# One edge-message kernel on Trainium2: the segment sums are issued ahead of the edge products on TensorE, and one wait goes

## The reference

```
h   = max(layernorm(x), 0)                        # 12500 x 48
tmp = concat([h[dst], h[src], edge_attr], 1)      # 400000 x (48 + 48 + 32)
msg = relu(tmp @ W1 + b1) @ W2 + b2               # hidden width 128
x  += segment_sum(msg, dst, num_segments=12500)
```

## Time and profile before

| | |
|---|---|
| median of three runs | 4776.21 us (4758.83 to 4780.47) |
| the profiled execution's own time | 4776.21 us |
| its span | 4774.3 us |
| TensorE busy, share of the span | 82% |
| GpSimd busy, share of the span | 55% |
| VectorE, ScalarE busy | 54%, 43% |
| mean granted TensorE clock, share of full | 0.85 |

### The profile page before, as it was taken

One profiled execution on the slowest core, in us unless ns is written; L12 is line 12 of the kernel. 1 busy time (PEld: TensorE's weight loads), 2 busy tenths in 40 slices (PEclk: granted clock), 3 DMA queues, 4 the chain that ended last, 5 costly groups with the idle time before them and its releaser, 6 DMA issues.

```text
span 4774.3 us, 95161 instructions
## 1 busy us (share of the span) xinstructions
PE 3927.4 (82%) x21992; PEld 3397.9 (71%) x21992; DVE 2554.6 (54%) x5906; ACT 2043.4 (43%) x7414; POOL 2613.2 (55%) x2766
## 2 busy tenths in 40 slices
PE   3788888888888888888888888888888888888887
PEld 3677777777777777777777777777777777777776
DVE  3655555565555555555555555555555555555553
ACT  2444444444444444444444444444444444444443
POOL 5455555555555555555555555555555555555555
PEclk9988888888888888888888888888888888888886
DMA  4522222222222222222222222222222222222223
GB/s 146 142 80 72 75 78 79 78 78 75 76 77 76 78 74 75 76 78 76 76 75 74 77 77 77 76 76 73 77 74 77 75 77 73 78 75 79 74 79 81
DMA packets 286658, 380.47 MB, mean 80 GB/s; under 512 B 90916, under 2 KB 190549, under 8 KB 285542
## 3 DMA queue, kind: packets, MB, share of 16 engines
q0 software_dynamic: 88064, 177.91, 14.7%
q1 hardware_dynamic: 198342, 201.58, 14.6%
q10 hardware_dynamic: 208, 0.49, 0.1%
HBM read 362.58 MB, written 17.04 MB: 80 GB/s over the span
## 4 chain that ended last, share of the span: by engine, by line
another core or an unknown queue 30%; issue 19%; DVE 18%; PE 14%; DVEq 11%; SPq 4%; ACT 4%; DMA 1%; ACTq 0%
PE ps L1310 6%; DVEq L1004 5%; DVE lhs L992 5%; PE ps L1286 3%; PE ps L1294 3%; DVE gath L1001 2%; DVE work L1047 2%; DVE onehot L979 2%; DVE p_hot L1025 2%; ACT work L674 2%; DVE nodes L1014 2%; SPq L411 1%; SPq L412 1%; DVEq L1093 1%
## 5 line engine op out<-in xcount | busy, mean ns | idle before, releaser
L535 POOL DMA_INDIRECT gath<-b_table,idx x2688 | 2549.3, 948 | 2127.3 <-ACT idx L639 1294.6
L1310 PE MATMUL ps<-h_tab,p_hot 128*128 128x480 f32 (+1 forms) x6768 | 1944.0, 431 | 259.5 <-issue 255.7
L1310 PEld LDWEIGHTS ps<-h_tab,p_hot 128*128 128x128 f32 x6768 | 1449.9, 226 | 467.6 <-issue 344.3
L674 ACT ACTIVATE work<-ps,work 128x80 f32<-128x80 f32 x4136 | 1039.1, 408 | 1675.3 <-remote 1458.2
L1286 PE MATMUL ps<-rhs,lhs 96*128 96x128 f32 x5376 | 906.6, 316 | 270.1 <-DVE gath L1001 124.3
L1286 PEld LDWEIGHTS ps<-rhs,lhs 96*128 96x128 f32 x5376 | 785.3, 219 | 403.1 <-issue 331.8
L1014 DVE TENSOR_TENSOR nodes<-ps,nodes 48x48 f32 x768 | 153.7, 200 | 1611.5 <-remote 1490.1
L1294 PE MATMUL ps<-onehot,gath 128*128 128x48 f32 x5376 | 799.6, 295 | 88.4 <-ACT gath L655 75.0
L1294 PEld LDWEIGHTS ps<-onehot,gath 128*128 128x128 f32 x5376 | 783.1, 221 | 109.1 <-ACT gath L655 95.0
L1025 DVE TENSOR_TENSOR p_hot<-work,ps 128x1152 fp32r<-128x1152 f32 x376 | 506.6, 1347 | 57.7 <-PE ps L1310 34.0
L992 DVE TENSOR_SCALAR_CACHE_REDUCE lhs<-nodes 48x512 f32<-48x512 f32 (+1 forms) x768 | 520.0, 677 | 32.0 <-issue 5.7
(11 more groups left out here) (128 smaller groups left out, 1640.8 us busy)
## 6 DMA issues: line engine op xcount, KB each, us to landing
nodes<-dst_row SPq DMA_DIRECT2D x494, 96.0 KB
gath<-b_table,idx POOLq DMA_INDIRECT x2688
nodes<-dst_row SPq DMA_DIRECT2D x384, 72.0 KB
lhs<-in_edge_t SPq DMA_DIRECT2D x384, 64.0 KB
work<-key_row SPq DMA_DIRECT2D x94, 256.0 KB
lhs<-in_edge_t SPq DMA_DIRECT2D x384, 48.0 KB
rhs<-a_table SPq DMA_DIRECT2D x768, 24.0 KB
work<-in_edge_t SPq DMA_DIRECT2D x220, 32.0 KB
```

The lines of the kernel that those rows point to most:

```text
L535: pool.indirect_dma_start(gath[:, u, t, :], None, b_table, bass.IndirectOffsetOnAxis(ap=idx[:, u, t:t + 1], axis=0)).then_inc(gathered[u], 16)
L674: m = nc.scalar.activation(p_sel[:, t % 2, :, at_j], ps_run[:, q, j * words:(j + 1) * words], ACT.Copy, scale=p_mask[:, at_j, t:t + 1])
L1310: mm = nc.tensor.matmul(ps_run[:, q, 0:m * words].rearrange("p (j w) -> p j w", j=m), p_hot[:, t % 2, i, :], h_tab[:, first:first + BLOCKS ...
```

## The change

On TensorE alone: in every step `make_sums` is issued ahead of `make_z` instead of behind it, and so are `make_sums_tail` of the early tiles and `turn_p` where j is 3. `make_z` no longer waits for `z_added`: `make_sums` of the same step, now ahead of it, waits for `r_ready` of the same step two before, which ScalarE signals after it has waited for that `z_added`.

```
@@ make_z
                 pe.wait_ge(hott_ready, s + 1)
-                if k >= 2:
-                    pe.wait_ge(z_added, s - 1)
                 for t in range(step_tiles(k)):
@@ cycle
                     k = LEAD + c * PERIOD + j
-                    make_z(k - 1, it)
                     make_sums(k - 3, it)
                     if j == 3 and ends_e:
                         make_sums_tail(place_e(c - 1, it))
                     if j == 3 and not first:
                         turn_p(c - 1, it)
+                    make_z(k - 1, it)
                     if j == 1 and ends_e:
                         make_z_tail(place_e(c - 1, it))
@@ after the last cycle
             for k in range(fetched, fetched + 3):
+                make_sums(k - 3, 0)
                 if k == fetched:
                     make_z(k - 1, 0)
-                make_sums(k - 3, 0)
                 if k % 2 == 0:
                     fold(k - 3, 0)
```

## The result

The changed kernel takes 4955.5 us (median of four runs, 4940.9 to 4962.33), the kernel before 4778.34 us beside it (4758.83 to 4783.35): 1.0394 of before, 95% interval 1.0348 to 1.0442, so 3.9% slower. The forecast was 4910 us with a range of 4765 to 5000. The profiled execution of after is on the long side: 4993.92 us with a span of 4992.1, where the thirteen executions of it on record lie between 4933.52 and 4995.9.

What follows compares the result with a forecast made beforehand. It took the late TensorE semaphores behind seven gathers a pair to bound the kernel. More long pairs gave +145 us by means, +122 by medians, taken as +135, other terms 0: 4776.2 became 4910 us, range 4765 to 5000.

Steps and rivals of the forecast that it cites:

- the release: TensorE's semaphores of a pair's second half come late, bunched about 1.5 us after the last gather's issue, setting pair length.
- The delay of the wide run and its effect on the choice of the way: Even j: uncovered rectification wait moves the wide run 0.55 us later (mean), so 19% of pairs are short, not 53%.
- the table of shares: For 295 wide runs: share followed by a short wait, by the run's end against the group of four's end.
- The short pairs: Wide run's semaphore precedes the release, so `pick` is done; GpSimd idles 2.74 us, mean pair 11.24; 177 to become 68.
- The third kind: Pairs whose idle time stands before the group of three, mean 13.05 us; forecast to fall from 37 to 20.
- long: ScalarE does the wide run's `pick` after the release; GpSimd idles 4.06 us, mean pair 12.64; 165 to become 291.
- The odd j's order: Changed order inside the stretch waiting for the release; four-tile sums 1.0 us sooner in the list; taken as 0.
- The removed wait: TensorE's wait for `z_added` before the product: bounds 0 to 8 us, taken as 0.
- the gathers decide alone: Rival: clock or gather phase decides whether the semaphore slips through; no change, about 4775 us, chance 0.14.
- the sums' semaphore counts: Rival: `take_idx` waits for four-tile sums, now sooner; faster, 4605 or milder 4733, between them 4690 us; chance 0.16.
- the clock falls further: Part of the everything-long rival: added TensorE idleness ahead of an even j lowers its clock, more late runs; 5015 us.
- everything long or of the third kind: Rival: all 359 other pairs long, 5015 us, or the third kind everywhere, 5165 us; chance 0.10.

Runs made afterwards that it cites:

- experiments 5 to 9: Semaphores held: the changed kernel again 1.0317 of before, delay_alone 1.0231, index_first 1.0058, even_only 1.0228, odd_only 1.0180.
- 10 to 12: Semaphores not held: the kernel before with one gather in each group of three 0.9294 of before, both_orders 1.0281, ahead_of_release 1.0000.
- 1 to 4: Semaphores not held: even_only 0.9999 of before, odd_only 0.9998, delay_alone 1.0000, index_first 0.9998.
- delay_alone: Kernel before, TensorE's order kept, but an even j's product waits for `r_ready` instead of `z_added`; 1.0231 of before held, 1.0000 not held.
- experiment 6: delay_alone with semaphores held, 4985.66 us against 4867.53; its table sorts wide runs by end against the group of four, with the share followed by short pairs.
- odd_only: Kernel before with the changed order in odd j only, `z_added` wait kept; 1.0180 of before held, 0.9998 not held.
- experiment 8: even_only with semaphores held: 4981.43 us, 1.0228 of before.
- index_first: Kernel before with ScalarE's index copy of an even j moved ahead of `pick` in the odd j before; 1.0058 held, 0.9998 not held.
- even_only: Kernel before with the changed order in even j only, `z_added` wait kept; 1.0228 of before held, 0.9999 not held.
- both_orders: even_only and index_first in one kernel, run only not held: 3571.27 us, 1.0281 of before.
- ahead_of_release: both_orders plus three-tile addition and rectification moved into the odd j, and TensorE waits ahead of `fold`; not held, 3474.73 us, 1.0000 of before.

## Why the prediction was right, and where it was not

*The bound.* Right for the condition that it was read from: the semaphores of TensorE come in a bunch behind the gathers, and GpSimd's next seven gathers hang on them. In the profile of after `fold`'s semaphore comes 1.5 to 1.8 us behind the end of the last gather's issue in 253 of the 357 cases that the trace has, and in these a median of 0.39 us behind the end of the last packet of the gathers' queue. That ties the release to the gathers' landing in time, not yet as its cause: no run took gathers away where the semaphores are held. The new thing is that this is a condition and not a property of the program: the same file runs at 3474 us without it. Why the semaphores are held stays open. That one chip does it and another not is not the answer, for experiments 5 to 9 and 10 to 12 ran on a chip of the same number (1 to 4 on another).

*The delay of the wide run and its effect on the choice of the way.* Right, and shown: the delay alone gives 1.0231 of the changed kernel's 1.03 to 1.04, and the table of shares under experiment 6 moves as forecast. That was the step that I trusted least. The delay was 0.80 us in the middle in after where I had 0.51; by itself the even j's part is 0.55, and the rest seems to come with the odd j's order, as the 2.70 of odd_only against 2.39 suggests (two sessions). TensorE's waits for the rectification grew by 164 us, within the 100 to 200 forecast; GpSimd's for the index copy grew to 1527, not to 1430.

*The counts.* The short pairs fell to 34, not to 68. The third kind rose from 37 to 90, not down to 20. The reason that I gave for its fall, the earlier sums of three tiles, holds for the even j's alone (none of the third kind in experiment 8); the odd j's order overrode it. With before's durations the measured counts give 4780 us for the 379 pairs, the forecast ones 4704; of these 76 us (by unrounded sums), 48 are the 34 short pairs fewer (34 x 1.40) and 28 are 70 pairs that are of the third kind instead of long (70 x 0.41). With their own durations it is 4770, +212 to before's 4558, against +218 between the spans. The forecast was +135, and the medians say +177.

*The odd j's order, costed at nothing to a gain.* Wrong, and the main miss: by itself it costs 1.8%. The total came as near as it did partly by luck: the +135 us, 2.8%, were for the even j's part, which by itself measured 2.3%, and what that was too high stood in for some of the term put at nothing. I had argued that what it moves is covered by the release, so that the earlier sums of four can only help. They come 1.0 us sooner in the list, and the more often their semaphore slips through before the release, the sooner the group of four follows the group of three without a gap; then the release falls behind the four, and finds the narrow run's `pick` there. That the odd j's order makes the third kind is in the counts: 90, 102 and 186 in the three profiles of kernels with it where the semaphores are held, 37, 41 and 0 in those with the old one and ScalarE's order unchanged; that the earlier sums are the reason is argued, from index_first, where an index copy of the four that is earlier for another reason does the same (270 pairs).

*The removed wait*, costed at 0: it had no run of its own, and even_only, odd_only and delay_alone all keep a wait there, so that it is worth nothing is not shown.

*The rivals.* That the gathers decide alone is refuted by the delay alone, which leaves the gathers as they are and costs 2.3%. That the sums' semaphore counts and makes the kernel faster has its sign wrong; its mechanism is half right if the account of the third kind above holds, for then the earlier sums do get their index copy sooner. That the clock falls further is seen (0.85 to 0.83 in the mean), but the even j's part costs its 2.3% without a lower clock. And everything long or of the third kind did not come: 34 pairs stayed short. Where nothing is held the window of even_only has TensorE busy for 468.53 of 500 us at 1.00, where after has it busy for 81% of the span at 0.83. The Trainium skill, "TensorE: Matmul & The Clock Gate", Part 1, has idleness lower the clock; the two conditions agree with that.

## What to carry to other kernels

Where an index copy or a load stands in one stream behind the reader of another engine's result, an edit elsewhere acts through which of the two is first in the queue when a late semaphore arrives; count the cycles by that first instruction, not by the mean wait. A cover of half a microsecond, here a product that ran beside a rectification, is worth keeping even on an engine that is not the bound. And before an order is tuned by tenths of a microsecond, time the kernel in several sessions: here one differs from another by 1400 us, and on the fast one five of the six kernels with another order or wait take the same time to 0.1%, and the sixth, both_orders, is 2.8% slower.

## What was not expected of the hardware

- One program took 3474 us or 4780 to 4870 us, steady within each session, with the same time in the gathers' packets (712 and 719 us) and the same issue time of a gather (0.95 us). In the slower one one in ten of `fold`'s semaphores came 5.9 us (after) or 6.4 us (before) behind its recorded end, in the other they came at 0.01 to 0.02. I don't know the cause.
- In the profiles of all kernels where the semaphores are held, and in that of both_orders, GpSimd pauses once in every 105 gathers inside a group, 25 times in the edge loop, in most of them for 2.07 us. It is 51 us in before and 50 in after, so no part of the difference. The profile names nothing that ends the pause, and the five profiles in which the gathers follow each other without a gap (even_only, odd_only, delay_alone and index_first where nothing is held, ahead_of_release) have none.
